# First mixture of a Flamingo block pair as one program: norms, routing and shared expert joined, rows transposed in pairs, the highest logit found in five steps, the norm chain begun in the attention

## What is computed

```python
mu, var = x.mean(-1), ((x - mu) ** 2).mean(-1)
h = (x - mu) / sqrt(var + 1e-5) * ln_gamma + ln_beta
shared_out = silu(h @ sw1.T) @ sw2.T            # ternary weights, 256 -> 512 -> 256
probs = softmax(h @ router_w.T)                 # 8 experts
top_prob, top_idx = probs.max(-1), probs.argmax(-1)
routed_out = top_prob * expert[top_idx](h)      # same shape as the shared expert
x = x + tanh(g_ffn[0]) * (shared_out + routed_out)
```

## Time and profile before

| | us |
|---|---|
| median of 3 runs | 1166.22 |
| lowest, highest | 1163.2, 1166.77 |
| the profiled execution | 1168.03 |
| its span, first to last instruction | 1166.3 |
| TensorE busy | 991.6 (85%) |
| VectorE busy | 774.0 (66%) |
| ScalarE busy | 595.6 (51%) |
| GpSimd busy | 249.1 (21%) |
| mean granted clock of TensorE | 0.911 |

### The profile page before, as it was taken

The page is one execution under the profiler, slowest core; times in us unless marked ns, Lnnn a source line. Parts: engine busy times, 40 slices in busy tenths (PEclk is TensorE's granted clock), DMA queues, the critical chain, the costliest instruction groups (busy, mean ns, idle before and its releaser), DMA issues. The chain is left out here.

```text
span 1166.3 us, 23301 instructions
## 1 busy us (share of the span) xinstructions
PE 991.6 (85%) x8394; PEld 919.4 (79%) x8394; DVE 774.0 (66%) x1978; ACT 595.6 (51%) x1439; POOL 249.1 (21%) x343
## 2 busy tenths in 40 slices
PE   4799998775799767999999999999977993699992
PEld 3687887565787556989999999999877893689992
DVE  5677777575766657878677776766767760356655
ACT  2476675242387525555555555555446430366660
POOL 3434433115000350010101001010000027125542
PEclk8799999757899878999999999999998995799997
DMA  8411111001056230101011010103040002325417
GB/s 253 139 52 57 56 39 38 1 1 69 26 164 165 69 84 5 44 1 43 1 44 43 1 43 1 43 10 106 1 109 1 1 26 110 122 89 171 136 62 248
DMA packets 75213, 77.94 MB, mean 67 GB/s; under 512 B 19681, under 2 KB 66273, under 8 KB 74977
## 3 DMA queue, kind: packets, MB, share of 16 engines
q1 hardware_dynamic: 68992, 62.33, 17.1%
q0 software_dynamic: 4992, 13.90, 3.4%
q10 hardware_dynamic: 1120, 0.27, 0.2%
HBM read 46.53 MB, written 29.95 MB: 66 GB/s over the span
## 5 line engine op out<-in xcount | busy, mean ns | idle before, releaser
L1491 PE MATMUL a_psK<-a_kvThi,a_wk 128*128 128x512 f32 x256 | 98.4, 425 | 2.8 <-DVE a_kvTlo L1671 1.4
L307 POOL TENSOR_SCALAR t_neg<-t_raw,t_nthr 128x256 bf16<-128x256 f32 (+1 forms) x54 | 60.8, 1142 | 112.0 <-DVE t_nthr L498 112.0
L1992 PE MATMUL f_psH<-m_turned,a_wq 128*128 128x256 f32 x384 | 60.9, 311 | 28.0 <-issue 24.5
L1992 PEld LDWEIGHTS f_psH<-m_turned,a_wq 128*128 128x128 f32 x384 | 55.4, 215 | 31.1 <-issue 31.1
L1548 PE MATMUL a_psY<-a_nwhi,a_uhi 128*128 128x256 f32 x256 | 73.8, 288 | 5.1 <-DVE a_ulo L1704 5.1
L1598 ACT ACTIVATE a_probs<-a_psS,a_nmax 128x256 f32<-128x256 f32 x128 | 59.6, 471 | 29.4 <-DVE a_nmax L1686 29.4
L1655 POOL TENSOR_TENSOR a_toklo<-a_kv,a_tokhi 128x512 fp32r<-128x512 f32 x16 | 22.1, 1382 | 243.2 <-ACT a_tokhi L1583 243.2
L1531 PE MATMUL a_psU<-a_pThi,a_tokhi 128*128 128x256 f32 x256 | 72.4, 283 | 0.0
L1531 PE MATMUL a_psU<-a_pTlo,a_tokhi 128*128 128x256 f32 x256 | 72.4, 283 | 0.0
L1531 PE MATMUL a_psU<-a_pThi,a_toklo 128*128 128x256 f32 x256 | 72.4, 283 | 0.0
L1548 PE MATMUL a_psY<-a_nwlo,a_uhi 128*128 128x256 f32 x256 | 72.3, 282 | 0.0
(11 more groups left out here) (366 smaller groups left out, 3260.0 us busy)
## 6 DMA issues: line engine op xcount, KB each, us to landing
t_raw<-in_L_ffn_expert_w SPq DMA_DIRECT2D x16, 512.0 KB, 3.9
f_raw<-in_fc_T SPq DMA_DIRECT2D x16, 512.0 KB, 3.8
m_turned<-m_sorted SPq DMA_DIRECT2D x8, 680.0 KB, 5.1
m_sorted<-a_zeros SPq DMA_DIRECT2D x8, 640.0 KB, 3.6
m_results<-a_zeros SPq DMA_DIRECT2D x8, 512.0 KB, 4.6
m_sorted<-m_zeros SPq DMA_DIRECT2D x1, 3072.0 KB, 13.0
e_xin<-m_sorted SPq DMA_DIRECT2D x24, 128.0 KB, 2.4
m_expert_out<-e_y SPq DMA_DIRECT2D x24, 128.0 KB, 1.7
```

Source lines behind the costliest of these rows:

```text
L307: ins = pool.tensor_scalar(neg[:, own], raw[h % NRAW][:, own], nthr[h % 2][:, n:n + 1], None, ALU.is_lt)
L1491: ins = pe.matmul(psK[:].rearrange("p b t -> p (b t)"), wk[x][:, a, h * DH:(h + 1) * DH], kvT[pair % 2][y][:, a, :, :, :].rearrange("p b m ...
L1992: ins = pe.matmul(psH[q][:, j * 2 * P:(j + 1) * 2 * P], w1[x][:, a, t * P:(t + 1) * P], hT[y_][:, a, tiles, :].rearrange("p b t -> p (b t) ...
```

## The change

1. The norm chain over `x` and context (16 steps) is issued in the attention: eight steps in its step 17, eight in step 18, on VectorE between `magnitudes` and `statistics`. At that point the statistics of the last tiles are not there, so a second chain over tiles 13 to 15 alone is issued between the rows of the new row loop.
2. `token_norms`, `route_top1` and `shared_ternary` become one function, `front_0`, with one block. Rows are normalized straight into `n_sb` (no copy by GpSimd) and transposed, scaled and scored by pairs of tiles. The high part is now copied by ScalarE, the low part is one 128x512 subtraction. All logits lie in one half of a PSUM bank and are taken out by one copy. `up(0)` and `up(1)` are issued between the transposes, after those of pairs 3 and 5.
3. The highest logit and its index come from five steps on 128x128 tensors instead of 16 + 16 instructions for single tiles. The softmax's denominators are made later, between parts of the shared expert.
4. In the shared expert ScalarE makes the high part too, and the two additions of a pair become one. ScalarE's order is all rows, Silu of pairs 0 and 1, Exp, then the loop of Silus. VectorE's is rows, choose, split(0), place, split(1), scale, owners, the results of pair 0. The scatter starts when `pos` is there (`placed`).

```diff
+                    if t > NB:
+                        for n in range((t - NB - 1) * 8, min((t - NB) * 8, norm_length(1))):
+                            k.step(norm_step(dve, n, *both))
                     if there(t - 1):
                         dve.bn_stats(c_stats[:, t - 1, :], ctx_sb[:, t - 1, :])
                     if there(t - 3):
                         statistics(t - 3)
...
-            token_norms(nc, sb, ps, sem, NB, D, KD, x_sb, ident, x_mean, x_rstd, both, n_sb, hT,
-                        logits, router, gamma, beta, NE, "m0", NB)
-            route_top1(nc, sb, ps, sem, NB, NE, NT, D, logits, prob, pos, owner, ones, upper, gates, cleared)
-            shared_ternary(nc, sb, ps, sem, NB, D, KD, KF, SH, hT, w1t, w2t, s1, s2, gates, x_sb, n_sb, pos, xg, scattered)
+        front_0(nc, sb, ps, sem, NB, NT, D, KD, KF, NE, x_sb, ident, gates, x_stats, x_mean, x_rstd, nt, NB - 3, n_sb,
+                prob, pos, owner, w1t, w2t, s1, s2, gamma, beta, router, ones, upper, xg, scattered, cleared)
...
             @block.gpsimd
             def _(pool):
+                pool.wait_ge(s["placed"], 1)
                 for i in range(NB):
                     pool.indirect_dma_start(xg, bass.IndirectOffsetOnAxis(ap=pos[:, i:i + 1], axis=0), n_sb[:, i, :], None)\
                         .then_inc(scattered, 16)
...
             @block.tensor
             def _(pe):
+                def turn(i):
+                    pe.wait_ge(s["row_done"], 2 * i + 2)
+                    at_least(pe, s["h_done"], i - SLOTS + 1)
+                    for a in range(KD):
+                        for b in range(2):
+                            ins = pe.transpose(psN[i % SLOTS][:, a, b, :], n_sb[:, 2 * i + b, a * P:(a + 1) * P], ident[:])
+                    ins.then_inc(s["turned"], 1)
+                def score(i):
+                    pe.wait_ge(s["h_done"], i + 1)
+                    for b in range(2):
+                        for a in range(KD):
+                            ins = pe.matmul(psL[:, 2 * i + b, :], h[i % SLOTS][:, a, b, :], router[:, a, :], start=(a == 0), stop=(a == KD - 1))
+                    ins.then_inc(s["scored"], 1)
...
+                turn(0)
+                turn(1)
+                for i in range(2, PAIRS):
+                    score(i - 2)
+                    turn(i)
+                    if i in (3, 5):
+                        b = (i - 3) // 2
+                        pe.wait_ge(s["h_lo"], b + 1)
+                        up(b, b, True)
+                score(PAIRS - 2)
+                score(PAIRS - 1)
+                pe.wait_ge(s["hot_done"], 1)
...
+                down(0, 0, True)
+                up(2, 0)
+                down(1, 1)
+                up(3, 1)
...
             @block.scalar
             def _(act):
+                def stage_rows(i):
+                    act.wait_ge(s["turned"], i + 1)
+                    at_least(act, s["scored"], i - SLOTS + 1)
+                    at_least(act, s["h_lo"], i - SLOTS + 1)
+                    for a in range(KD):
+                        ins = act.activation(h[i % SLOTS][:, a, :, :], psN[i % SLOTS][:, a, :, :], ACT.Identity, bias=beta[:, a:a + 1],
+                                             scale=gamma[:, a:a + 1])
+                    ins.then_inc(s["h_done"], 1)
+                    act.wait_ge(s["h_done"], i + 1)
+                    act.activation(hT[0][:, :, pair(i), :], h[i % SLOTS][:], ACT.Copy).then_inc(s["h_hi"], 1)
...
+                for i in range(PAIRS):
+                    stage_rows(i)
+                silu(0, 0, True)
+                silu(1, 1, True)
+                act.wait_ge(s["shifted_done"], 1)
+                act.activation(expd[:], shifted[:], ACT.Exp).then_inc(s["exp_done"], 1)
                 with act.Fori(1, PAIRS // 2) as i:
                     for b in range(2):
                         silu(i * 2 + b, b)
...
             @block.vector
             def _(dve):
+                def choose():
+                    dve.wait_ge(s["scored"], PAIRS)
+                    dve.tensor_copy(logits[:], psL).then_inc(s["logits_out"], 1)
+                    dve.wait_ge(s["logits_out"], 1)
+                    k.step(dve.tensor_reduce(top[:], logits[:], AX.X, ALU.max))
+                    k.step(dve.tensor_tensor(match[:], logits[:], by_token(top[:]), ALU.is_equal))
+                    k.step(dve.tensor_tensor(match[:], match[:], by_expert(under[:]), ALU.mult))
+                    k.step(dve.tensor_reduce(which[:], match[:], AX.X, ALU.min))
+                    dve.tensor_tensor(hot[:], by_token(which[:]), by_expert(under[:]), ALU.is_equal).then_inc(s["hot_done"], 1)
...
+                rows_in()
+                dve.wait_ge(s["iota_done"], 1)
+                dve.tensor_scalar(under[:], iota_i[:, 0:NE], float(-NE), None, ALU.add)
+                k.step(dve.tensor_copy(iota[:], iota_i[:]))
+                choose()
+                split(0, 0, True)
+                end = place()
+                split(1, 1, True)
                 dve.tensor_scalar(s2g[:], s2[:, SH, :], gates[:, 2:3], None, ALU.mult).then_inc(s["s2g"], 1)
                 dve.wait_ge(s["s2g"], 1)
...
+                owners(end)
+                dve.wait_ge(s["down"], 2)
+                for j in range(2):
+                    dve.tensor_tensor(y[:, j, :], psY[j][:, 0, :], s2g[:], ALU.mult).then_inc(s["kept"], 1)
+                dve.wait_ge(s["kept"], 2)
+                dve.tensor_tensor(x_sb[:, 0:2, :], x_sb[:, 0:2, :], y, ALU.add).then_inc(s["added"], 1)
                 split(2, 0)
                 keep(1)
+                probabilities()
                 split(3, 1)
```

More of the change, by code:

```diff
@@ new lines, in front_0 @@
+        psY = [ps(f"s0_psY{i}", [P, 2, D], F32, c) for i in range(2)]
+        psL = psY[0][:, 1, 0:NB * NE].rearrange("p (b e) -> p b e", e=NE)
+        psR = psN[0][:].rearrange("p a b t -> p (a b t)")[:, 0:2 * NB * NE].rearrange("p (n b e) -> p n b e", n=2, e=NE)
+        names = ("steps row_done turned h_done h_hi h_lo scored logits_out iota_done hot_done ranked shifted_done exp_done placed "
+                 "up silu g_hi g_lo down kept added s2g").split()
+        s = {n: sem(f"f0_{n}", c) for n in names}
@@ L887, in _ @@
                 recycle(nc, pool, cleared)
-            @block.scalar
-            def _(act):
-                act.wait_ge(s["shifted_done"], 1)
-                act.activation(expd[:], shifted[:], ACT.Exp).then_inc(s["exp_done"], 1)
-            @block.tensor
-            def _(pe):
-                pe.wait_ge(s["hot_done"], 1)
-                flat = hot[:].rearrange("p b e -> p (b e)")
-                pe.matmul(psR[:, 0, :], upper[:], flat, start=True, stop=True)
-                pe.matmul(psR[:, 1, :], ones[:], flat, start=True, stop=True).then_inc(s["ranked"], 1)
@@ L1010, in silu @@
                         ins.then_inc(s["silu"], 1)
-                silu(0, 0)
-                silu(1, 1)
+                    for q in range(NQ):
+                        own = slice(2 * q, 2 * q + 2)
+                        act.wait_ge(s["silu"], i * NQ + q + 1)
+                        if not first and q == 0:
+                            act.wait_ge(s["down"], (i - 1) * 2)
+                        act.activation(gs[b][0][:, own, :], g[b][:, own, :], ACT.Copy).then_inc(s["g_hi"], 1)
+                for i in range(PAIRS):
[4 more added lines that the diff above has]
+                act.activation(expd[:], shifted[:], ACT.Exp).then_inc(s["exp_done"], 1)
                 with act.Fori(1, PAIRS // 2) as i:
@@ L1019, in _, with row @@
             def _(dve):
-                def split(i, b):
-                    at_least(dve, s["down"], (i - 1) * 2)
+                k = Steps(dve, s["steps"])
+                late = slice(normed_ahead, NB)
+                norms = (x_stats[:, late, :], x_mean[:, late], x_rstd[:, late], [t[:, late] for t in nt], NB - normed_ahead)
+                def row(b):
+                    dve.tensor_scalar(n_sb[:, b, :], x_sb[:, b, :], x_mean[:, b:b + 1], x_rstd[:, b:b + 1],
+                                      ALU.subtract, ALU.mult).then_inc(s["row_done"], 1)
@@ new lines, in lower, with rows_in @@
+                def lower(i):
+                    dve.wait_ge(s["h_hi"], i + 1)
+                    dve.tensor_tensor(hT[1][:, :, pair(i), :], h[i % SLOTS][:], hT[0][:, :, pair(i), :].bitcast(F32), ALU.subtract)\
+                       .then_inc(s["h_lo"], 1)
+                def rows_in():
+                    steps, ahead = norm_length(1), normed_ahead // 2
+                    for i in range(PAIRS):
+                        for b in range(2):
+                            row(2 * i + b)
+                            for n in range(steps * (2 * i + b) // (2 * ahead), min(steps * (2 * i + b + 1) // (2 * ahead), steps)):
+                                k.step(norm_step(dve, n, *norms))
+                        if i >= SLOTS:
+                            lower(i - SLOTS)
```

(2 more changed lines are left out.)

274 lines of the change are left out of this document (76 added, 198 removed).

## The result

The changed kernel takes 1151.64 us in the median of 4 runs (1149.80 to 1153.15), the kernel before 1166.1; the ratio is 0.988 (95% interval 0.9857 to 0.9903), so 11 to 17 us faster. The profiled execution took 1149.80, with a span of 1148.0.

The account below looks back on a forecast made before the run. Gains lie in the norm chain, routing and TensorE's idleness, with TensorE bounding the new row loop. Stage end 297.3 + 10.6 + 0.8 = 308.7 against 316.4, say 8 us earlier: 1158, range 1147 to 1165.

Parts of the forecast that it names:

- Part 1: Norm chain moved into attention steps 17 and 18: first row 1.0 us earlier; the late rows' second chain hides under TensorE.
- Part 2: Row loop by pairs, TensorE-bound at 1.2 GHz, with up(0) and up(1) inside: 30.0 us, last score at 260.65.
- rival (a): Row loop: TensorE's clock rises within it, 6 us more gain than forecast, 1152; chance 0.20.
- Part 3: Choosing and placing: one-hot starts 1.65 us after the last score, placing takes 5.0 us, scatter begins at about 269.1.
- Part 4: Shared expert: new 2.2 us wait before down(1), 12 units in 22.9 us, tail of 2.2, end 297.3 before scatter loss.
- The loss under the scatter: Shared expert: TensorE held up while GpSimd issues 16 indirect DMAs; kept at 10.6 us, bounds 0 and 19.
- rival (b): Shared expert: the scatter costs little, 10 us more gain than forecast, 1148; chance 0.08.
- Rival (c): Shared expert: ScalarE becomes the loop's bound through a table load in all three passes, 1.3 us a pass, 1162; chance 0.14.
- the table switches: Exp between Silus on ScalarE: two new loads of 1.28 us each, falling between 266.0 and 269.0, cost nothing.
- (d): Shared expert: TensorE never gets back to 2.4 GHz, 16 us lost, so 8 slower, 1174; chance 0.05.
- (e): Shared expert: loss under the scatter grows by 5 to 8 us, so no difference, 1164; chance 0.08.

Follow-up runs that it names:

- e5: Changed kernel with the norm chain out of the attention again, all 16 steps alone ahead of the first row, no second chain: 1151.41 us.
- e4: Changed kernel with up(0) and up(1) taken out of the row loop and issued behind the two rank products: 1124.97 us, ratio 0.9972 (chip 5).
- e10: Changed kernel with GpSimd waiting after 8 of 16 indirect DMAs until four pairs are added, second run on chip 5: 1120.57 us, ratio 0.9914.
- e11: Changed kernel with Exp behind the Silu loop, pair 0's kept output before split(1) and owners, scatter bursts of 6, 5, 5: 1121.01 us, ratio 0.9922 (chip 5).
- e2: Changed kernel with GpSimd waiting after 8 of 16 indirect DMAs until four pairs are added, first run on chip 5: 1118.20 us, ratio 0.9915.
- e12: Changed kernel with GpSimd waiting after 8 of 16 indirect DMAs until four pairs are added, run on chip 13: 1153.56 us, ratio 0.989.
- e6: Changed kernel with the old 16 maxima and 16 index operations in place of the five steps: 1153.12 us (chip 10).
- e3: Changed kernel with ScalarE's Exp and the softmax denominators moved behind the Silu loop: 1119.17 us (chip 5).
- the pause: Changed kernel with GpSimd waiting after 8 of 16 indirect DMAs until four pairs are added: 1118.20 and 1120.57 us on chip 5, 1153.56 on chip 13.
- e1: Changed kernel with one indirect DMA in place of the first mixture's 16: 1119.82 us, ratio 0.9923 (chip 5).

## Why the prediction was right, and which term was not

**The verdict and the range held**: faster, 1151.6 within 1147 to 1165. The likeliest number, 1158, was 6.4 too high.

**Part 1 held**: first row 8.98 forecast, 9.03 measured. That the second chain "hides under TensorE" was not quite so: without it e5 is 0.6 us shorter behind the first row, 0.34 of it ahead of up(0).

**Part 2 is the term that was mis-sized.** "21.7 + 6.8 + 1.5 = 30.0" took 1.2 GHz for the whole loop. From the first row to the one-hot operand I had 31.65 us; it took 24.02, 7.6 less, which is nearly all of the 8.2 us at the end. By the positions the forecast had the changed kernel 0.5 us behind the old one; it was 6.7 ahead. The clock rose 12.7 us after the first row. This is rival (a), given 0.20 and 1152. e4 shows its cause by its absence: without the 32 dense products the clock stays at 0.50 for the whole loop. My evidence against it was that the old loop, 89% busy, stayed at 0.50; but that loop has no dense run of 256-column matmuls in it, and it could not speak on one that has. So the 7.6 are two things: 23.39 measured without the products, and 6.8 for them, make 30.2, which is 1.4 less than my sum at 1.2 GHz; the other 6.2 are the clock, the 6 of rival (a). Nor is the gain a fixed one: ten profiles have up(0) and up(1) in the loop. In all of them up(0) runs from 8 to 12 us after the first row. In eight the clock rose 11.9 to 12.8 us after it, in e10 and e11 only at 19.7 and 20.1, near the end of up(1). e10 is the same kernel as e2 and e12, so the edits don't decide it, and what does was not found. It costs e10 3.6 us up to the one-hot operand and 3.2 up to the positions:

```profile
228.50:241.50 13.00, 11.64 (x54) 11.03 (x55) 9.83 (x37) 6.49 (x12) 0.15 (x1) 0.50 0.00 1
241.50:256.00 14.50, 12.81 (x75) 12.55 (x75) 4.82 (x13) 9.22 (x18) 0.00 (x0) 0.62 0.00 1
```

**Part 3**: the five steps bring 2.6 us (e6) and hand back 0.5 through split(0) in front of the totals. Totals to positions 4.82 us, forecast 5.0.

**Part 4**: the new wait for the kept output is there, 2.12 for 2.2. Its sum without the scatter, 22.9 + 2.2 + 0.8 of small gaps from 260.87, less the 0.7 of the last addition, starts that at 286.1, 28.3 us behind the positions; e3, with no wait and no table loads, measured 28.22. The loss under the scatter was put at 10.6. Against 29.15 us on chip 5, the five profiles with the changed shared expert and 16 indirect DMAs on other chips show 9.0, 11.3, 10.2 (e5), 9.4 (e6) and, with the pause, 9.7 more. So the size of this very stage was the right one to take, and rival (b), no loss, is what happens on another chip.

**Rival (c) was half right.** The loads do stand in each pass of the loop, as in the three rows above. By the Trainium skill (ScalarE activation tables: per-element evaluation and per-set limits, Table sets in the compiler and the runtime) loads are placed per block; the trace agrees, in that each pass of the loop executes one. But I priced them at 1.3 us a pass; e3 shows 0.93 in all up to the last addition, and where the scatter holds TensorE up that part was not measured. So "nothing" for the table switches was off by 0.9. That the copies moved to ScalarE cost nothing held, by the 28.22 us above. The drain beside each load that the Trainium skill gives (ScalarE: Activation LUTs, What ACT_TABLE_LOAD costs) is not to be seen here either: the load of 254.73 ends at 256.01 and Exp starts at 256.03.

**(d) and (e)** did not happen: the clock is 1.00 in the last stretch, and the loss under the scatter, 9.0 us by the comparison above, did not grow over the 10.6.

**In part luck**: the median lies on the 1152 of rival (a), but that had 6 us more than the forecast for the clock alone. The stage gave 8.2 more, and what follows it, counted at nothing, took 1.4 more, in a stretch that spreads from 849.9 to 854.5 over the profiles off chip 5.

**What stays open.** On chip 5 the variants that should equal the changed kernel there (e1, e2, e10) are 8 to 10 us ahead of the kernel before; in the two sessions elsewhere the changed kernel is 14.4 and 14.5 ahead. The changed kernel loses about 10 us under the scatter; for the kernel before to lose 5 more would explain it, but no profile of it without the wait exists, and the medians also hold the second mixture's wait, which was not taken apart. And what holds TensorE's events back on chips 10 and 13 but not on 5 was not found.

## What to carry to other kernels

Dense matmuls moved into a loop that runs at 1.2 GHz can pay for themselves by lifting the clock for what follows; that the old loop was busy and stayed low did not tell, so give that case its own sum, and look at more than one profile. When another function stands just ahead of a loop of Silus, look for a table load in every pass; but before moving it out, look where the next load will then stand: here it moved to the head of the next stage. And before chasing a wait that the profile calls remote or issue, run the kernel on a second chip.

## What the runs showed of the hardware

- The wait under indirect DMAs belongs to the chip or the session: both sessions on chip 5 lack it, those on chips 10 and 13 have it. The same eight-pair loop with the same 16 indirect DMAs takes 29.1 us on chip 5 and 38 to 40 on others; in the second mixture ScalarE waits 41.09 us in the changed kernel's first profile, and e2 on chip 5 has no such wait. The pause kernel, one and the same program, takes 1118.20 and 1120.57 us on chip 5 and 1153.56 on chip 13; about 10 us of that difference lie in the first mixture behind the positions (38.83 for 29.14 and 29.15), 24 to 27 behind its last addition.

```profile
981.57 0.84 ACT L2062 ACTIVATE f_g<-f_psH,m_bs 128x256 f32<-128x256 f32 x2 [41.09 <-remote]
```

- Where it exists, TensorE's own first gap comes 10 to 15 us after the first indirect DMA. ScalarE's last wait ends 1.0 to 2.9 us after the last one has ended in the first mixture, 4.5 in the second. TensorE's events are late before its own gap: in e12 already behind a burst of 11 us. A rest of 7.6 us cleared it.
- The clock's rise in the row loop came 12.7, 12.8 and 19.7 us after the first row for one and the same kernel (e12, e2, e10); the late one cost 3.2 us by the positions.
- A table load takes 1.28 us, and the instruction behind it starts 0.02 us after its end (254.73, 256.01, 256.03).
